# Turning the gated expert products by DMA instead of TensorE in a six-stage transformer block on one core

## The chip, the cores and the metric

One core of a Trainium2 chip runs the whole program. The metric is device time in microseconds (us), the median of three executions. The engines are TensorE (PE, matrix products and transposes into PSUM, with PEld for its weight loads), VectorE (DVE), ScalarE (ACT), GpSimd (POOL) and SyncE (SP, which only issues transfers here). They run their own instruction lists and meet at semaphores.

## The reference, cut to what matters

Six stages follow each other on 2048 tokens of 128 numbers: a ternary feed-forward stage, attention, feed-forward, a mixture of experts, a second attention, and the mixture of experts once more. The change touches only the two mixtures. Each token goes to its two best of eight experts, weighted by a softmax `w` over the two logits:

```python
xs = X[:, :, None, :] * w[..., None]
for e in range(E):
    h = silu(einsum('btsd,dh->btsh', xs, W1[e])) * einsum('btsd,dh->btsh', xs, W3[e])   # H = 512
    y = einsum('btsh,hd->btsd', h, W2[e])
    out = out + where(topi == e, y, 0).sum(axis=2)
```

## The kernel before

**Precision.** Every float32 operand of a product is split into a float16 high part and a float16 low part (the float32 value less the high part), and a product is three matmuls: high by high, high by low, low by high.

**Tiles.** In each mixture (called `moe(0)` and `moe(1)`) the 4096 token copies are sorted by expert into tiles of 128 rows. With padding there are `ETILES` = 46 tiles, 23 for each half of the tokens (`HT`), so 92 tiles in all. GpSimd gathers the rows of a tile from `x_rows` in HBM (L835) and scatters its results into `y_rows` (L843). The expert of a tile is read into registers.

**A tile's path.** (1) `gather` fills `XG`, a ring of 4. (2) `turned_token`, L2103: TensorE turns it; ACT (L1116) and DVE (L1652) write high and low parts. (3) `up`, L1698 to L1700: six matmuls of 512 columns, three into bank 1 (the W1 product), three into bank 2 (W3). (4) `gate`, L1124: ACT writes silu of bank 1 to `SA`; `product`, L1662: DVE multiplies bank 2 by it and writes float32 `G32`, 128 tokens by 512. (5) `turned_product`, L2128: four float32 transposes on TensorE put the product into bank 3 or 4, since `down` needs the 512 hidden numbers on partitions. (6) `product_high` (ACT, L1130) and `product_low` (DVE, L1668) split it out of PSUM. (7) `down`, L2140 to L2142: twelve matmuls of 128 columns into bank 5. (8) `result`, L1138: ACT copies it to `YS`, a ring of 4, and GpSimd scatters it.

**Order.** Each engine's list is written by hand. `run_tiles` goes through turns; in turn `t` a stage with lag `k` handles tile `t-k`, by `TLAGS = (0, 1, 2, 3)`: token, up and gate and product, turned product and split, down and result. So TensorE's turn is token(t), up(t-1), turned product(t-2), down(t-3). GpSimd's turn `u` is gather(u), then scatter(u-8). `carried` adds other work to a turn: the rest of the feed-forward stage, routing of the second half of the tokens, and, in turns 24 to 38 of `moe(0)`, `second_turned`, which turns weights of the second attention.

**SP's list.** It loads weights, writes normed tokens to `x_rows` (L610) and, when a half is scattered, reads `y_rows` back in four transfers (L618).

Of the kernel before, what the change touches and what calls it, by code (L numbers as in the profile page):

```python
# [19 lines left out]
F32 = mybir.dt.float32  # L20
# [11 lines left out]
def macaron_block(nc: bass.Bass, ins, out, phases):  # L32
    tokens = ins["L0_attn_tokens"]
    NB, SEQ, D = tokens.shape
    P = 128
# [32 lines left out]
    with ctx:  # L68
# [74 lines left out]
        GRING = 3  # L143
        XRING = 4
        YRING = 4
# [79 lines left out]
        YS = carve([YRING, D], F32)  # L225
# [7 lines left out]
        GL = carve([GRING, HB, P], F16)  # L233
        G32 = carve([2, H], F32)
        GH = carve([GRING, HB, P], F16)
# [137 lines left out]
        s_gt_ps = sem("gt_ps")  # L373
# [4 lines left out]
        s_y_out = [sem("y_out0"), sem("y_out1"), sem("y_out2"), sem("y_out3")]  # L378
# [4 lines left out]
        def moved(m, slot, t):  # L383

            return 16 * (m * ((ETILES + XRING - 1 - slot) // XRING) + (t + XRING - 1 - slot) // XRING)
# [146 lines left out]
        TLAGS = (0, 1, 2, 3)  # L532
        OUT_LAG = 8

        def run_tiles(m, stages, carried):

            for t in range(ETILES + TLAGS[-1]):
                for f, lag in zip(stages, TLAGS):
                    if f is not None and 0 <= t - lag < ETILES:
                        f(t - lag, ETILES * m + t - lag)  # L540
                carried(m, t)

# [14 lines left out]
        def _(sp):  # L557
# [18 lines left out]
            for i, (src, hi, lo) in enumerate(experts):  # L576
# [12 lines left out]
            sp.wait_ge(s_lo_pool, 2 + 4 * len(experts))  # L589
            flat = stage[:].rearrange("p a b -> p (a b)")  # L590
            sp.dma_start(flat[:, 0:3 * INNER].rearrange("p (c d) -> p c d", d=D), wqkv1).then_inc(s_w1_in, 16)
            sp.dma_start(flat[:, 3 * INNER:4 * INNER], wout1).then_inc(s_w1_in, 16)

            def end_loads():

                for k in range(YRING):
                    sp.wait_ge(s_y_out[k], moved(1, k, ETILES))
# [8 lines left out]
            def moe(n, m):  # L606
                for c in range(NCH):
                    sp.wait_ge(s_ln_xn, NORM_NO[n, c])
                    at = c % HCH * CH
                    sp.dma_start(x_rows[c // HCH][at:at + CH].rearrange("(p t) d -> p t d", t=TPC),  # L610
                                 XN[:, TPC * c:TPC * (c + 1), :]).then_inc(s_x_rows[c // HCH], 16)
                for h in range(PARTS if m == 0 else 1):
                    for k in range(YRING):
                        sp.wait_ge(s_y_out[k], moved(m, k, HT * (h + 1)))
                    for c in range(HCH * h, HCH * (h + 1)):
                        for j in range(TOPK):
                            at = j * TOK + c * CH
                            sp.dma_start(Yt[:, c, j],  # L618
                                         y_rows[at:at + CH].rearrange("(p t) d -> p t d", t=TPC)
                                         ).then_inc(s_y_got[c], 16)  # L620
                    if m == 1:
                        stored(h)

            x_out = out.rearrange("b (t p) d -> p (b t) d", p=P)

            def stored(h):

                for c in range(HCH * h, HCH * (h + 1)):
                    sp.wait_ge(s_x_moe, TOPK * (NCH + c + 1))
                    sp.dma_start(x_out[:, TPC * c:TPC * (c + 1), :], X[:, TPC * c:TPC * (c + 1), :]  # L630
                                 ).then_inc(s_out_done, 16)
            moe(3, 0)
            moe(5, 1)
# [7 lines left out]
        def _(pool):  # L641
# [125 lines left out]
            def attention(a, turns=range(TURNS)):  # L767

                def body(t):
                    p, m, s, v, o = items(t)  # L770
                    if s is not None:
                        j = ITEMS * a + s
                        b = s & 1
                        for u in range(3 if s < ITEMS - 1 else 2):
# [85 lines left out]
        def _(act):  # L860
# [248 lines left out]
            def moe(m):  # L1109
# [8 lines left out]
                def gate(t, w):  # L1118
# [5 lines left out]
                    a_.activation(SA[:, t % 2, :], ps[:, 1, :], ACT.Silu, scale=wup[:, t:t + 1]).then_inc(s_a_sb, 1)  # L1124

                def product_high(t, w):
                    act.wait_ge(s_gt_ps, w + 1)
                    if t >= GRING:
                        act.wait_ge(s_y_ps, w - GRING + 1)
                    a_.activation(GH[:, t % GRING].rearrange("p a b -> p (a b)"), ps[:, 3 + t % 2, :], ACT.Copy  # L1130
                                  ).then_inc(s_g_hi, 1)

                def result(t, w):
                    k = t % YRING
                    act.wait_ge(s_y_ps, w + 1)
                    if t >= YRING:
                        act.wait_ge(s_y_out[k], moved(m, k, t))
                    a_.activation(YS[:, k, :], ps[:, 5, 0:D], ACT.Copy, scale=0.5 / W_UP).then_inc(s_y_sb, 1)  # L1138
                run_tiles(m, (token_high, gate, product_high, result), carried)
# [6 lines left out]
            for k in range(YRING):  # L1146
                act.wait_ge(s_y_out[k], moved(1, k, ETILES))
# [11 lines left out]
        def _(dve):  # L1159
# [488 lines left out]
            def moe(m):  # L1648
# [6 lines left out]
                def product(t, w):  # L1655
# [4 lines left out]
                    if t >= 2:  # L1660
                        dve.wait_ge(s_gt_ps, w - 1)
                    v_.scalar_tensor_tensor(G32[:, t % 2, :], ps[:, 2, :], wup[:, t:t + 1], SA[:, t % 2, :], ALU.mult,  # L1662
                                            ALU.mult).then_inc(s_g32_rdy, 1)

                def product_low(t, w):
                    g = t % GRING
                    dve.wait_ge(s_g_hi, w + 1)
                    v_.tensor_tensor(GL[:, g].rearrange("p a b -> p (a b)"), ps[:, 3 + t % 2, :],  # L1668
                                     GH[:, g].rearrange("p a b -> p (a b)"), ALU.subtract).then_inc(s_g_lo, 1)
                run_tiles(m, (token_low, product, product_low, None), carried)  # L1670
# [498 lines left out]
```

## Time and profile before

| | us |
|---|---|
| median of 3 runs | 967.55 (967.09 to 970.55) |
| span of the profiled execution | 1000.9 |
| `moe(0)`, first gather to last scatter in that span | 360.9 to 530.5 |
| `moe(1)`, its turns from 4 on, to the last scatter | 845.8 to 990.0 |

The page gives no other time of the profiled execution than its span, which is 3.4% above the median of the runs. Times inside the span are compared with the span, and a difference is scaled by 967.55/1000.9 = 0.967 at the end. How to read it: an engine's busy share is an average; in the two mixtures all engines work at once, and what matters is how far apart the tiles follow each other.

### The profile page before, as it was taken

Reading aid. Unit: us, or ns where it says so; the run is one execution under the profiler, and the core shown is the slowest. Engines: PE = TensorE matmul, PEld = TensorE weight load, DVE = VectorE, ACT = ScalarE, POOL = GpSimd, SP = SyncE. Lnnn points to the kernel's source line nnn. Section 1 sums busy time; section 2 is a strip of 40 time slices with the busy share of each in tenths; the row PEclk is TensorE's granted clock in tenths of the full one; section 3 lists DMA queues with packets and bytes.
Section 4 is the critical chain, followed back from the end, with each engine's and each line's share of the span. In section 5 each row is a group of like instructions: output and inputs, shape, how many; then the busy total and the mean of one; then the engine's idle time right before and its main releaser. Section 6 shows DMA issues by size and latency. Waiting matters only on the chain.

```text
span 1000.9 us, 33897 instructions
## 1 busy us (share of the span) xinstructions
PE 897.1 (90%) x13160; PEld 640.5 (64%) x13160; DVE 792.1 (79%) x2394; ACT 673.5 (67%) x1183; POOL 734.7 (73%) x685
## 2 busy tenths in 40 slices
PE   5789999999999879899987899999999985998884
PEld 3467676776777656566654676777677764666663
DVE  6889898888889877777656889888888887866563
ACT  6688888878877626556555787767767762545552
POOL 6789989889887745666545999878888883666662
PEclk9999999999999979999999999999999997999997
DMA  5201011010030001122111000000000001121222
GB/s 153 78 10 45 3 45 45 3 45 2 3 107 3 2 20 39 52 43 85 38 30 51 3 3 3 12 3 2 13 3 3 13 2 30 41 43 44 86 62 82
DMA packets 21118, 33.79 MB, mean 34 GB/s; under 512 B 4578, under 2 KB 10466, under 8 KB 20964
## 3 DMA queue, kind: packets, MB, share of 16 engines
q1 hardware_dynamic: 13728, 18.50, 5.9%
q0 software_dynamic: 5888, 12.07, 4.8%
q8 instruction: 110, 1.80, 0.8%
q10 hardware_dynamic: 1348, 1.05, 0.3%
q14 instruction: 44, 0.36, 0.1%
HBM read 22.44 MB, written 9.18 MB: 32 GB/s over the span
## 4 chain that ended last, share of the span: by engine, by line
PE 63%; DVE 18%; ACT 6%; issue 6%; POOL 3%; another core or an unknown queue 2%; DMA 1%; SPq 0%; POOLq 0%; DVEq 0%; ACTq 0%
PE ps L1698 8%; PE ps L1889 8%; PE ps L1700 8%; PE ps L1699 7%; DVE arena L1308 4%; PE ps L1919 3%; PE ps L2128 3%; PE ps L1853 3%; PE ps L1920 3%; PE ps L1921 3%; PE ps L2140 2%; PE ps L2141 2%; PE ps L2142 2%; PE ps L1864 2%
## 5 line engine op out<-in xcount | busy, mean ns | idle before, releaser
L784 POOL TENSOR_TENSOR arena<-arena 128x1024 f16<-128x1024 f32 x190 | 344.9, 1816 | 86.2 <-ACT arena L980 75.9
L1308 DVE CUSTOM_DVE_ANT_0 arena<-ps,mask_qk 128x512 bf16<-128x512 f32 (+3 forms) x512 | 224.4, 485 | 25.0 <-PE ps L1853 23.8
L972 ACT ACTIVATE arena<-ps,lift 128x1024 f32<-128x1024 f32 (+1 forms) x192 | 186.7, 972 | 85.0 <-PE ps L1899 82.2
L1889 PE MATMUL ps<-arena 64*128 64x512 f16 (+3 forms) x1536 | 148.5, 299 | 10.2 <-ACT arena L972 6.8
L835 POOL DMA_INDIRECT arena<-x_rows,arena x92 | 92.6, 1006 | 88.5 <-PE ps L2103 43.7
L1919 PE MATMUL ps<-arena 128*128 128x65 f16 x1280 | 130.9, 195 | 0.2 <-DVE arena L1332 0.2
L1920 PE MATMUL ps<-arena 128*128 128x64 f16 x1280 | 130.4, 193 | 0.0
L1921 PE MATMUL ps<-arena 128*128 128x65 f16 x1280 | 130.0, 194 | 0.0
L843 POOL DMA_INDIRECT y_rows<-arena x92 | 90.8, 987 | 49.0 <-ACT arena L1138 26.1
L1919 PEld LDWEIGHTS ps<-arena 128*128 128x128 f16 x1280 | 117.4, 98 | 8.4 <-issue 0.5
L1920 PEld LDWEIGHTS ps<-arena 128*128 128x128 f16 x1280 | 117.9, 99 | 0.2 <-issue 0.2
L1921 PEld LDWEIGHTS ps<-arena 128*128 128x128 f16 x1280 | 117.9, 98 | 0.0
L782 POOL CAST arena<-arena 128x1024 f16<-128x1024 f32 x124 | 103.6, 835 | 0.0
L1662 DVE SCALAR_TENSOR_TENSOR arena<-ps,arena 128x512 f32<-128x512 f32 x92 | 68.8, 748 | 29.1 <-ACT arena L1124 16.0
L1889 PEld LDWEIGHTS ps<-arena 64*128 64x128 f16 x1536 | 52.1, 94 | 53.1 <-ACT arena L972 22.3
L1668 DVE TENSOR_TENSOR arena<-ps,arena 128x512 f16<-128x512 f32 x92 | 63.1, 686 | 26.1 <-ACT arena L1130 18.4
L1130 ACT ACTIVATE arena<-ps 128x512 f16<-128x512 f32 x92 | 55.3, 601 | 42.1 <-PE ps L2128 24.7
L2140 PE MATMUL ps<-E2h,arena 128*128 x368 | 71.4, 222 | 11.1 <-DVE arena L1668 6.0
L1124 ACT ACTIVATE arena<-ps,arena 128x512 f32<-128x512 f32 x92 | 63.4, 689 | 18.5 <-PE ps L1700 15.1
L1853 PE MATMUL ps<-arena 64*128 64x512 f16 (+3 forms) x512 | 66.2, 296 | 7.7 <-DVE arena L1308 6.6
L2142 PE MATMUL ps<-E2h,arena 128*128 x368 | 71.1, 219 | 0.0
L2141 PE MATMUL ps<-E2l,arena 128*128 x368 | 71.0, 219 | 0.0
(288 smaller groups left out, 2695.9 us busy)
## 6 DMA issues: line engine op xcount, KB each, us to landing
stage<-in_L_ffn_W SPq DMA_DIRECT2D x4, 1024.0 KB, 5.3
arena<-y_rows SPq DMA_DIRECT2D x14, 256.0 KB, 3.6
x_rows<-XN SPq DMA_DIRECT2D x8, 256.0 KB, 2.1
arena<-x_rows,arena POOLq DMA_INDIRECT x92
y_rows<-arena POOLq DMA_INDIRECT x92
stage<-in_L_attn_Wkv SPq DMA_DIRECT2D x2, 512.0 KB, 8.3
X<-in_L_attn_tokens SPq DMA_DIRECT2D x3, 256.0 KB, 5.1
out_x<-X SPq DMA_DIRECT2D x3, 256.0 KB
```

The lines of the kernel that those rows point to most:

```text
L782: g.tensor_copy(PH[:, b, :, cols], P32[:, :, cols]).then_inc(s_ph_pool, 1)
L784: g.tensor_tensor(PL[:, b, :, cols], P32[:, :, cols], PH[:, b, :, cols], ALU.subtract).then_inc(s_pl, 1)
L835: g.indirect_dma_start(XG[:, t % XRING, :], None, x_rows[t // HT], bass.IndirectOffsetOnAxis(ap=row_i[:, 0, t:t + 1], axis=0)).then_inc(s_ ...
L972: a_.activation(P32[:, :, UNIT_AT[u]:UNIT_AT[u] + UNIT_W[u]], ps[:, 4:6, 0:UNIT_W[u]], ACT.Exp, bias=lift[:]).then_inc(s_ex_p, 1)
L1308: v_.tensor_tensor_reduce(masked[:, x, 0:w], ps[:, 2 + x, at:at + w], mask_qk[:, CH - w:CH], 1.0, NEG, ALU.add, ALU.max, accum_out=MX[:, i ...
L1853: ins_ = mm(ps[:, 2 + x, at:at + (i + 1) * P], QKh[rows, r, 0, i * P:(i + 1) * P], QKh[rows, r, 1, 0:(i + 1) * P], start=(n_ == 0), stop=( ...
L1889: mm(ps[:, 4 + x, at:at + w], keys, queries, start=(n_ == 0 and part == 0), stop=False)
L1919: mm(ps[:, 6 + x, c:c + DH + 1], ph_, VH[:, r, k, x, 0:DH + 1], start=(k == 0), stop=False)
L1920: mm(ps[:, 6 + x, c:c + DH], ph_, VL[:, r, k, x, :], start=False, stop=False)
L1921: ins_ = mm(ps[:, 6 + x, c:c + DH + 1], pl_, VH[:, r, k, x, 0:DH + 1], start=False, stop=(k == i))
L2140: mm(dst, GH[:, g, f, :], wh, start=(f == 0), stop=False)
L2142: ins_ = mm(dst, GL[:, g, f, :], wh, start=False, stop=(f == HB - 1))
```

## The change

The split now comes first and the turn second, and the turn is a transfer. ACT (`product_high`) and DVE (`product_low`) split `G32` from SBUF to SBUF, into `GS`, 128 by 1024 float16, a ring of 3 (`SRING`). SP issues one `dma_start_transpose` per tile, `GS` to `GT`, a ring of 4, 256 KB each. `down` reads `GT`, with a lag of 4 turns instead of 3. Banks 3 and 4, now free, make a second pair for `up` (`up_banks`). `YS` is a ring of 8 instead of 4. SP's list is rewritten so that its other transfers stand between the transposes. GpSimd's list has the same instructions; one wait on the last scatters is added in the second attention.

```diff
-        GRING = 3
+        GRING = 4
+        SRING = 3
-        YRING = 4
+        YRING = 8
...
-        TLAGS = (0, 1, 2, 3)
+        DOWN_LAG = 4
...
+        def up_banks(t):
+            return 1 + 2 * (t % 2), 2 + 2 * (t % 2)
...
+            def results_in(m, h):
+                for k in range(YRING):
+                    sp.wait_ge(s_y_out[k], moved(m, k, HT * (h + 1), YRING))
+                for c in range(HCH * h, HCH * (h + 1)):
+                    for j in range(TOPK):
+                        at = j * TOK + c * CH
+                        sp.dma_start(Yt[:, c, j], y_rows[at:at + CH].rearrange("(p t) d -> p t d", t=TPC)
+                                     ).then_inc(s_y_got[c], 16)
...
+            def moe(m):
+                for t in range(ETILES):
+                    w = ETILES * m + t
+                    sp.wait_ge(s_g_lo, w + 1)
+                    if t >= GRING:
+                        sp.wait_ge(s_y_ps, w - GRING + 1)
+                    sp.dma_start_transpose(GT[:, t % GRING].rearrange("p k f d -> p (k f) d"),
+                                           GS[:, t % SRING].rearrange("p k h -> p (k h)")
+                                           ).then_inc(s_g_turned[t % GRING], 16)
...
+                    if t == 31:
+                        results_in(m, 0)
...
                 def product_high(t, w):
-                    act.wait_ge(s_gt_ps, w + 1)
-                    if t >= GRING:
-                        act.wait_ge(s_y_ps, w - GRING + 1)
-                    a_.activation(GH[:, t % GRING].rearrange("p a b -> p (a b)"), ps[:, 3 + t % 2, :], ACT.Copy
+                    act.wait_ge(s_g32_rdy, w + 1)
+                    if t >= SRING:
+                        act.wait_ge(s_g_turned[(t - SRING) % GRING], moved(m, (t - SRING) % GRING, t - SRING + 1))
+                    a_.activation(GS[:, t % SRING, 0], G32[:, t % 2, :], ACT.Copy).then_inc(s_g_hi, 1)
...
-                run_tiles(m, (token_high, gate, product_high, result), carried)
+                run_tiles(m, ((token_high, 0), (product_high, 2), (gate, 1), (result, DOWN_LAG)), carried)
...
                 def product_low(t, w):
-                    v_.tensor_tensor(GL[:, g].rearrange("p a b -> p (a b)"), ps[:, 3 + t % 2, :],
+                    v_.tensor_tensor(GS[:, t % SRING, 1], G32[:, t % 2, :], GS[:, t % SRING, 0], ALU.subtract
-                run_tiles(m, (token_low, product, product_low, None), carried)
+                run_tiles(m, ((token_low, 0), (product_low, 2), (product, 1)), carried)
...
-                    if t >= 1:
-                        pe.wait_ge(s_a_sb, w)
+                    if t >= 2:
+                        pe.wait_ge(s_a_sb, w - 1)
...
-                def turned_product(t, w):
-                    for f in range(HB):
-                        ins_ = nc.tensor.transpose(ps[:, 3 + k, f * P:(f + 1) * P], G32[:, k, f * P:(f + 1) * P], ident[:])
...
                 def down(t, w):
-                    pe.wait_ge(s_g_lo, w + 1)
+                    pe.wait_ge(s_g_turned[g], moved(m, g, t + 1))
...
-                run_tiles(m, (turned_token, up, turned_product, down), carried)
+                run_tiles(m, ((turned_token, 0), (up, 1), (down, DOWN_LAG)), carried)
```

TensorE's list in a turn of `moe(1)` before: token, the six up matmuls, the four transposes of the product, and then the first of the down matmuls (`arena` holds all tile buffers, `ps` is PSUM).

```order
L2103 MATMUL ps<-ident,arena 128x128 [waits t_lo,xg_in2]
L1698 ISA [waits a_sb,t_lo]
L1698 MATMUL ps<-E1h,arena 128x512
...
L1700 MATMUL ps<-E1h,arena 128x512
L1698 REGISTER_ALU [waits g32_rdy]
L1698 MATMUL ps<-E3h,arena 128x512
...
L1700 MATMUL ps<-E3h,arena 128x512
L2128 MATMUL ps<-ident,arena 128x128 [waits g_lo,g32_rdy]
L2128 MATMUL ps<-ident,arena 128x128 x3
L2140 REGISTER_ALU [waits y_sb,g_lo]
L2140 MATMUL ps<-E2h,arena 128x128
```

The same turn in the changed kernel:

```order
L2156 MATMUL ps<-ident,arena 128x128 [waits t_lo,xg_in2]
L1751 ISA [waits a_sb,t_lo]
L1751 MATMUL ps<-E1h,arena 128x512
...
L1753 MATMUL ps<-E1h,arena 128x512
L1751 REGISTER_ALU [waits g32_rdy]
L1751 MATMUL ps<-E3h,arena 128x512
...
L1753 MATMUL ps<-E3h,arena 128x512
L2185 REGISTER_ALU [waits y_sb,g_turned2]
L2185 MATMUL ps<-E2h,arena 128x128
```

The four L2128 rows are gone, the waits on `a_sb` and `g32_rdy` are now for the tile before the last, and `down` waits for a transfer (`g_turned`).

SP's list through `moe(0)` and the read-back of its results before:

```order
L610 DMA x_rows<-XN 128x512 [waits ln_xn] x4
L618 DMA arena<-y_rows 128x512 [waits y_out2,y_out3,y_out1,y_out0]
L618 DMA arena<-y_rows 128x512 x3
```

And in the changed kernel:

```order
L665 DMA_TRANSPOSE arena<-arena 128x8x128 [waits g_lo] x4
L665 DMA_TRANSPOSE arena<-arena 128x8x128 [waits y_ps,g_lo]
L608 DMA x_rows<-XN 128x512 [waits ln_xn]
L665 DMA_TRANSPOSE arena<-arena 128x8x128 [waits y_ps,g_lo] x3
L608 DMA x_rows<-XN 128x512 [waits ln_xn]
L665 DMA_TRANSPOSE arena<-arena 128x8x128 [waits y_ps,g_lo] x24
L618 DMA arena<-y_rows 128x512 [waits y_out4,y_out5,y_out3,y_out6,y_out2,y_out7,y_out1,y_out0]
L618 DMA arena<-y_rows 128x512 x3
L665 DMA_TRANSPOSE arena<-arena 128x8x128 [waits y_ps,g_lo] x14
```

46 transposes now stand in this list, and the read-back of the first half is issued ahead of the last 14 of them.

## Rows read from the trace of the kernel before

**Rows 1.** The page: busy time of the engines over the span.

```profile
PE 897.1 (90%) x13160; PEld 640.5 (64%) x13160; DVE 792.1 (79%) x2394; ACT 673.5 (67%) x1183; POOL 734.7 (73%) x685
```

**Rows 2.** Stretches: busy us of each engine, granted clock, DMA share, GB/s.

```profile
440.00:493.00 53.00, 49.36 (x419) 35.34 (x418) 35.99 (x72) 31.17 (x77) 34.11 (x35) 1.00 0.21 63
882.00:969.00 87.00, 78.40 (x647) 54.27 (x645) 52.03 (x101) 45.80 (x113) 55.65 (x57) 1.00 0.23 59
...
850.00:860.00 10.00, 9.06 (x96) 6.53 (x95) 9.25 (x39) 5.66 (x13) 4.85 (x5) 1.00 0.12 35
```

**Rows 3.** Timeline of POOL: start, duration, line, idle before and releaser.

```profile
360.87 1.23 POOL L835 DMA_INDIRECT arena<-x_rows,arena  x1 [11.57 <-DVE arena L1515]
...
433.82 0.97 POOL L835 DMA_INDIRECT arena<-x_rows,arena  x1 [1.64 <-DVE arena L1515]
...
440.02 0.97 POOL L835 DMA_INDIRECT arena<-x_rows,arena  x1 [1.38 <-remote]
...
492.75 0.98 POOL L835 DMA_INDIRECT arena<-x_rows,arena  x1 [0.82 <-PE ps L2103]
...
498.33 0.24 POOL L661 TENSOR_SCALAR pw<-mv 128x4 f32<-128x4 f32 x1 [3.32 <-DVE mv L1177]
...
882.48 0.97 POOL L835 DMA_INDIRECT arena<-x_rows,arena  x1 [0.97 <-PE ps L2103]
...
902.79 0.99 POOL L843 DMA_INDIRECT y_rows<-arena  x1 [0.30 <-issue]
904.08 0.97 POOL L835 DMA_INDIRECT arena<-x_rows,arena  x1 [0.30 <-issue]
905.35 0.99 POOL L843 DMA_INDIRECT y_rows<-arena  x1 [0.30 <-issue]
...
968.87 1.11 POOL L835 DMA_INDIRECT arena<-x_rows,arena  x1 [0.30 <-issue]
...
989.06 0.96 POOL L843 DMA_INDIRECT y_rows<-arena  x1 [0.75 <-ACT arena L1138]
```

**Rows 4.** The chain that ended last, end of `moe(1)`: start, duration, what.

```profile
968.37 1.44 PE ps L1700
969.85 2.14 another core or an unknown queue
972.01 0.61 ACT arena L1130
...
976.25 0.44 PE ps L2128 x4
978.77 0.44 PE ps L2128 x4
981.29 0.44 PE ps L2128 x4
```

**Rows 5.** DVE, ACT and TensorE by line, medians of one.

```profile
L2103 PE MATMUL ps<-ident,arena x92: 272/299/454, 364.2 to 979.7; 128*128 128x128 f32 x92
L1130 ACT ACTIVATE arena<-ps x92: 588/597/633, 374.9 to 985.3; 128x512 f16<-128x512 f32 x92
L980 ACT ACTIVATE arena<-arena x64: 1045/1048/1082, 52.3 to 820.7; 128x1024 f16<-128x1024 f32 x64
L1668 DVE TENSOR_TENSOR arena<-ps,arena x92: 677/690/694, 375.5 to 985.9; 128x512 f16<-128x512 f32 x92
L1327 DVE TENSOR_TENSOR arena<-arena x2: 681/681/681, 352.6 to 829.2; 128x512 f16<-128x512 f32 x2
```

**Rows 6.** The page's issues: KB each, median us to landing.

```profile
arena<-y_rows SPq DMA_DIRECT2D x14, 256.0 KB, 3.6
x_rows<-XN SPq DMA_DIRECT2D x8, 256.0 KB, 2.1
...
stage<-in_L_attn_Wout SPq DMA_DIRECT2D x1, 512.0 KB, 8.9
```

**Rows 7.** The page's DMA queues: packets, MB, share of 16 engines.

```profile
q1 hardware_dynamic: 13728, 18.50, 5.9%
...
q8 instruction: 110, 1.80, 0.8%
```

More of the change, by code:

```diff
@@ L224, in macaron_block @@
         used[0] = ARENA - 1024
-        YS = carve([YRING, D], F32)
         tile_ei = carve([64], I32)
@@ L530, in macaron_block @@
         KEY_AT = {k: UNIT_AT[u] + at for u, unit in enumerate(EXP_UNITS) for k, at in unit}
-        TLAGS = (0, 1, 2, 3)
+        DOWN_LAG = 4
         OUT_LAG = 8
         def run_tiles(m, stages, carried):
-            for t in range(ETILES + TLAGS[-1]):
-                for f, lag in zip(stages, TLAGS):
-                    if f is not None and 0 <= t - lag < ETILES:
+            for t in range(ETILES + DOWN_LAG):
+                for f, lag in stages:
+                    if 0 <= t - lag < ETILES:
                         f(t - lag, ETILES * m + t - lag)
                 carried(m, t)
+        def up_banks(t):
+            return 1 + 2 * (t % 2), 2 + 2 * (t % 2)
         def second_weights(i):
@@ new lines, in attention, with body @@
+            def attention(a):
+                def body(t):
+                    if a == 0 and t == 0:
+                        expert_block(0)
+                    if a == 0 and t == 1:
+                        expert_block(1)
+                    if a == 0 and t in (6, 10, 14, 18):
+                        expert_block((t - 6) // 4 + 2)
+                    if a == 0 and t == 27:
+                        second_layer()
+                    if t in ROWS_OUT[a]:
+                        rows_out(*ROWS_OUT[a][t])
+                run_items(body, range(TURNS))
@@ L604, in end_loads @@
                              ).then_inc(s_out_done, 16)
[L606 to L622, printed above, removed]
@@ L624, in _, with stored @@
-            x_out = out.rearrange("b (t p) d -> p (b t) d", p=P)
[L626 to L633, printed above, removed]
+            x_out = out.rearrange("b (t p) d -> p (b t) d", p=P)
+            def stored(c):
+                sp.wait_ge(s_x_moe, TOPK * (NCH + c + 1))
+                sp.dma_start(x_out[:, TPC * c:TPC * (c + 1), :], X[:, TPC * c:TPC * (c + 1), :]
+                             ).then_inc(s_out_done, 16)
@@ L634, in _ @@
+            attention(0)
+            moe(0)
+            results_in(0, 1)
+            attention(1)
+            moe(1)
             end_loads()
@@ L773, in body @@
                         b = s & 1
+                        if a == 1 and s == 1:
+                            for k in range(YRING):
+                                pool.wait_ge(s_y_out[k], moved(0, k, ETILES, YRING))
                         for u in range(3 if s < ITEMS - 1 else 2):
```

79 lines of the change are left out of this document (47 added, 32 removed).

## The prediction

> **What bounds the kernel now.** I read the page first. TensorE is busy 90% of the span [rows 1], which invites the thought that 368 transposes off TensorE are worth their full time. The stretches come next. In the two quiet stretches of the mixtures, 440 to 493 and 882 to 969, TensorE is busy 93% and 90%, GpSimd 64%, DVE 68% and 60%, and the clock is full [rows 2]. So TensorE leads, but it is no plain TensorE bound, and the pace per tile says more.
>
> GpSimd's timeline gives that pace, since it gathers each tile once. From the gather at 882.48 to the last at 968.87 there are 28 steps, 3.09 us each; from 440.02 to 492.75 there are 17, 3.10 each [rows 3]. Two floors lie below. TensorE's undisturbed pace is the step of the L2128 group near the end of the chain: 976.25, 978.77, 981.29, or 2.52 us [rows 4]. GpSimd's own floor is a scatter, a gather and their gaps with nothing to wait for: 902.79 to 905.35, or 2.56 us [rows 3]. **So the kernel sits 0.5 us per tile above two floors that are almost equal.** The 0.5 us comes from stalls. The chain shows one: after L1700, 2.14 us of "unknown queue", before ACT's L1130 [rows 4]. I counted seven of this kind in `moe(1)`, about every fifth tile, and near each the instruction queue (110 fetches of 16 KB [rows 7]) moved a packet. Because the engines are tied closely (one bank pair, the turned product one turn after it is made), a stall of TensorE passes on to all, and at a 2.52 pace against 2.56 on GpSimd nothing can be caught up.
>
> **The change part by part.**
>
> *Removed: four transposes a tile.* Their group takes 0.44 us on TensorE's path [rows 4]. TensorE's floor becomes 2.52 - 0.44 = 2.08. The full price over 92 tiles would be 40 us, but GpSimd's 2.56 is untouched: its list is the same. So in steady stretches the new pace is GpSimd's 2.56, not 2.08, and the gain is 3.09 - 2.56: the slack of 0.48 lets TensorE catch up after a stall, which it could not do before.
>
> *ACT and DVE.* The high split reads SBUF: half of L980's 1048 ns for twice the columns is 524, against 597 for L1130; I take 560, between them [rows 5]. The low split becomes what L1327 does, 681 against 690 for L1668 [rows 5]. Both are hidden: with all four operations a turn costs about 1.8 us on either engine.
>
> *Added: a 256 KB transposing transfer per tile.* The trace of before has none. The bounds are 2.1 us to landing for the same bytes out of SBUF, and 8.9 us for 512 KB, so 4.45 for 256 [rows 6]. I take 3.6, the row of the same size that writes into SBUF. Time allowed: the low split of tile t-2 is done about 1.4 us into turn t, and `down` of that tile begins about 1.5 us into turn t+2 (token 0.2, up 1.3). That is two turns and a little, 5.2 us at 2.56. So 3.6 us is hidden with 1.6 to spare. Without the cover each us beyond 5.2 would cost half a us per tile, since it lies across two turns. Load on the DMA engines: q1 moved 18.5 MB in 5.9% of 16 engines' span [rows 7], so 256 KB takes 0.8 us of all sixteen; per 2.56 us that adds 0.33 to a share of 0.2 [rows 2]. The engines stay under 0.6.
>
> *Moved: SP's list.* Ahead of the transposes stand the four read-backs at t = 31 in each mixture and single `x_rows` writes. The scatters for which the read-backs wait are issued two turns earlier, so the wait is short. What is queued behind them is the next transpose, and TensorE's `down` behind that. Four read-backs of 256 KB add three landings' worth of bytes, about 3 x 1.1 us, against 1.6 to spare: 1.8 us, and twice that is 3.6; I take 4.
>
> *Second bank pair, `YS` ring of 8.* These only remove waits; they are part of the catching up. A ring of 8 lets ACT's result go on although a scatter lands late.
>
> *One more turn of lag.* It costs only at the ends, and is in the tail below.
>
> **The sum** (against the span of 1000.9):
> - `moe(1)` from 882.48: 28 steps from 3.09 to 2.56 (72 us instead of 86.4): -14.4. Lower bound 0, if the stalls stay on the path.
> - `moe(1)` tail: now 989.06 - 968.87 = 20.2 us from the last gather to the last scatter [rows 3], since TensorE is a ring of four tiles behind GpSimd. After, TensorE has kept up. The tile lands after 3.3 (first gather 360.87, first L2103 364.2 [rows 3, 5]), then token, `up` in the next turn, to 6.9; gate, product and both splits with gaps, 3.1; transfer 3.6; down, result, 1.1: 14.7. So -5.4.
> - `moe(1)` before 882: DVE has the routing and is busy 9.25 of 10 us [rows 2]; little can move. -2 (0 to -5).
> - `moe(0)`, 440 to 493: TensorE also turns weights here (one group of four, 0.44, per two turns: 0.22). Its floor is 2.08 + 0.22 + one stall of 2.14 per six tiles, 0.36, so 2.7, which exceeds GpSimd's 2.56. 17 x 0.4 = -6.8.
> - `moe(0)`, first half: 433.82 - 360.87 over 23 tiles is 3.17 [rows 3], with feed-forward and routing in between. Full price of the transposes 23 x 0.44 = 10; half of it, since DVE's routing decides when the second half may start (L1515 released both ends [rows 3]): -5 (0 to -10).
> - `moe(0)` end: GpSimd waited 3.3 us for DVE's L1177 because it ran four tiles ahead [rows 3], and TensorE's backlog is smaller: -4 (0 to -8).
> - read-backs ahead of transposes: +4 (0 to +10).
>
> Together -33.6 on the span, 967.3; times 0.967 is -32.5 on the median, so **935**. All gains at full, costs at nothing: about -49, or 920.
>
> **A page against it.** The landing of 2.1 to 3.6 us for 256 KB [rows 6] is for plain transfers. The Trainium skill, "VectorE: DVE Perf Modes", section "The three transpose paths", gives 390 ns for a 128 x 128 turn on TensorE and 1309 ns by the DMA crossbar. By an estimate from that page, eight such blocks one after another are 10.5 us a tile, and the sum would be about 680 us above the time of now. The same notes, "Advanced Engine Details and Errata", section "X-Bar Transpose (TRN2)", call transposing DMAs as fast as regular ones; by that my 3.6 would stand. No run so far shows either.
>
> **The rivals.**
> - *A, the forecast* (0.50): GpSimd's pace; 918 to 946.
> - *B, the stalls stay* (0.17). Transposes put 0.33 more load on the queues that also fetch TensorE's instructions. If a stall grows from 2.14 to 4 us, TensorE's pace is 2.08 + 4/6 = 2.75 and over 60 quiet tiles 11 us of the gain are lost; with the full cost of the read-backs another 6. About 951, span 946 to 962. For it: the fetch near each stall. Against: 0.48 us of slack a tile absorbs 2.14 in five tiles.
> - *C, no change* (0.08): the pace is set by something that neither floor shows, and a tile's longer path eats the rest; 963 to 972. The case that the change does not do what it says lies here too: the TensorE instructions are gone from its list, so only the gain can fail.
> - *D, slower* (0.25): the crossbar serves one tile after another, slower than tiles are made. Place: SP's queue; `down` waits on `g_turned`, then ACT's `product_high` for its ring of 3. Price: at 4.45 us a tile (the bound from 8.9 for 512 KB [rows 6]) 92 x (4.45 - 3.1) = +124, times 0.967: 1087. It decides from a pace of about 3.1 us on: below that A's gain only shrinks. For it: no row shows a transposing transfer, and each turned block ends as 256 bytes on every partition. Against: an ordinary 256 KB takes 0.8 us of the engines [rows 7]. The Trainium skill's block-by-block estimate above is the extreme of this case.
>
> **How the numbers follow.** 935 is A's value; A's own range is 918 to 946. Half of 1% is about what a measurement tells from no change. Faster by more than 0.5% are A and B and a sliver of C: 0.67. Within: 0.08. Slower: 0.25, of which I put about 0.1 below 1000. The range 916 to 1000 leaves out some 0.03 below and 0.15 above.
>
> **What would show it.** Right: gathers 2.56 to 2.6 apart in the quiet stretches, with "issue" before them and not L2103; TensorE idle about a fifth there; transposes landing within 5 us; scatter of the last tile about 15 us after the last gather. Wrong: TensorE or its `down` line waiting for the transfer (D), ACT's high split waiting for `g_turned` (D), steps still near 3 us with stalls of over 2 us in the chain (B), or a new releaser in front of GpSimd's gathers (C).

## The result and the profile after

The changed kernel takes 975.32 us (median of 8 runs, 969.81 to 978.13) against 968.18 for the kernel before on the same chip (8 runs). The ratio is 1.0068, 95% interval 1.0046 to 1.0090: **slower by 0.7%**, where 935 was forecast. The profiled execution has a span of 972.8 us and took 974.55.

The page of the changed kernel: engines (busy us, share), DMA queues (packets, MB, share of 16 engines), the costliest groups, and an issue row. They answer to [rows 1, 7, 6].

```profile
PE 862.8 (89%) x12792; PEld 599.9 (62%) x12792; DVE 788.3 (81%) x2394; ACT 672.1 (69%) x1183; POOL 742.9 (76%) x685
...
q1 hardware_dynamic: 110880, 42.63, 20.6%
...
L889 POOL DMA_INDIRECT arena<-x_rows,arena x92 | 94.6, 1028 | 50.9 <-issue 23.7
...
L2185 PE MATMUL ps<-E2h,arena 128*128 x368 | 74.4, 226 | 27.0 <-DMA arena<-arena 20.3
...
arena<-y_rows SPq DMA_DIRECT2D x14, 256.0 KB, 4.3
```

GpSimd's gathers now mostly wait for "issue", as forecast; but `down` (L2185) waits 20.3 us for the turned product, in places where TensorE has nothing else. The turning made 110880 packets of q1 out of 13728.

The line of the transfer, SP's L665: min, median and max of SP's own time for one issue in ns, and who waited for it (us, times).

```profile
L665 SPq DMA_TRANSPOSE arena<-arena x92: 1231/1233/3457, 376.1 to 956.0; - x92
...
  PE ps L2185: 20.3, 16
```

Stretches of the changed kernel, columns as in [rows 2]. The first is the quiet one, the others are short ones near its end.

```profile
870.00:928.00 58.00, 48.73 (x391) 30.73 (x390) 36.37 (x66) 31.90 (x83) 43.54 (x43) 0.96 0.86 167
...
926.00:930.00 4.00, 3.73 (x20) 2.23 (x21) 0.98 (x2) 1.70 (x4) 2.36 (x3) 0.57 0.82 191
939.00:943.00 4.00, 4.00 (x23) 2.25 (x23) 1.56 (x4) 1.65 (x4) 2.31 (x3) 0.62 0.89 187
```

The DMA engines are 86% busy. The second and third rows are granted clocks of 0.57 and 0.62, that is, mostly the lower of TensorE's two levels (1.2 against 2.4 GHz). The chain that ended last says what went before each: start, duration, what.

```profile
920.05 6.10 DMA arena<-arena
926.15 0.12 issue
926.27 0.26 PE ps L2185
...
927.93 0.43 PE ps L1751
928.35 0.43 PE ps L1752
...
932.53 0.60 DVE arena L1721
933.15 5.33 DMA arena<-arena
938.49 0.12 issue
...
953.92 2.72 DMA arena<-arena
```

The low split (L1721) ends, the transfer lands 5.33 us later, and `down` follows. Behind a landing of 6.10 us TensorE runs `up` at 0.43 us a matmul instead of 0.22. A late transfer near the end, when the gathers are over, takes 2.72. The chain shows only the late ones. By the semaphores of the trace, the transfers issued between 862 and 930 us land after 2.8 to 6.2 us, 3.9 in the middle (median).

GpSimd's timeline, columns as in [rows 3]:

```profile
894.35 0.97 POOL L889 DMA_INDIRECT arena<-x_rows,arena  x1 [0.30 <-issue]
895.63 0.99 POOL L897 DMA_INDIRECT y_rows<-arena  x1 [0.30 <-issue]
896.92 0.97 POOL L889 DMA_INDIRECT arena<-x_rows,arena  x1 [0.30 <-PE ps L2156]
...
941.65 0.97 POOL L889 DMA_INDIRECT arena<-x_rows,arena  x1 [0.30 <-issue]
944.25 0.98 POOL L897 DMA_INDIRECT y_rows<-arena  x1 [1.63 <-ACT arena L1192]
...
960.70 0.97 POOL L897 DMA_INDIRECT y_rows<-arena  x1 [1.28 <-ACT arena L1192]
```

Where nothing is late, gathers are 2.57 us apart. The tail from last gather to last scatter is 19.05 us, not the 14.7 of the sum.

### The profile page after: what moved, and what is told of

It reads as the page before. It is cut to its first block, busy times and chain, and to the rows that moved or that the text cites. A ratio compares the mean times of both kernels' runs of the same rounds, so it can differ in the third digit from the quotient of the medians.

```text
span 972.8 us, 33253 instructions
## 1 busy us (share of the span) xinstructions
PE 862.8 (89%) x12792; PEld 599.9 (62%) x12792; DVE 788.3 (81%) x2394; ACT 672.1 (69%) x1183; POOL 742.9 (76%) x685
## 3 DMA queue, kind: packets, MB, share of 16 engines
q1 hardware_dynamic: 110880, 42.63, 20.6%
## 4 chain that ended last, share of the span: by engine, by line
PE 56%; DVE 21%; DMA 8%; ACT 6%; issue 6%; POOL 3%; SPq 0%; POOLq 0%; DVEq 0%; ACTq 0%
PE ps L1942 8%; PE ps L1751 7%; DMA arena<-arena 7%; PE ps L1752 6%; PE ps L1753 6%; DVE arena L1362 4%; PE ps L1972 4%; PE ps L1906 3%; PE ps L1973 3%; PE ps L1974 3%; PE ps L2185 2%; PE ps L2186 2%; PE ps L1917 2%; PE ps L1982 2%; DVE arena L1721 2%
## 5 line engine op out<-in xcount | busy, mean ns | idle before, releaser
L897 POOL DMA_INDIRECT y_rows<-arena x92 | 95.0, 1033 | 55.2 <-ACT arena L1192 37.2
L889 POOL DMA_INDIRECT arena<-x_rows,arena x92 | 94.6, 1028 | 50.9 <-issue 23.7
L2185 PE MATMUL ps<-E2h,arena 128*128 x368 | 74.4, 226 | 27.0 <-DMA arena<-arena 20.3
L1192 ACT ACTIVATE arena<-ps 128x128 f32<-128x128 f32 x92 | 25.5, 277 | 79.2 <-PE ps L2187 73.7
L1721 DVE TENSOR_TENSOR arena<-arena 128x512 f16<-128x512 f32 x92 | 63.7, 692 | 15.3 <-ACT arena L1185 15.0
L2187 PE MATMUL ps<-E2h,arena 128*128 x368 | 73.7, 224 | 0.0
L2186 PE MATMUL ps<-E2l,arena 128*128 x368 | 73.5, 223 | 0.1
L2185 PEld LDWEIGHTS ps<-E2h,arena 128*128 128x128 f16 x368 | 36.5, 99 | 50.5 <-issue 41.6
```

Source lines behind the costliest of these rows:

```text
L889: g.indirect_dma_start(XG[:, t % XRING, :], None, x_rows[t // HT], bass.IndirectOffsetOnAxis(ap=row_i[:, 0, t:t + 1], axis=0)).then_inc(s_ ...
L897: g.indirect_dma_start(y_rows, bass.IndirectOffsetOnAxis(ap=row_i[:, 1, t:t + 1], axis=0), YS[:, t % YRING, :], None).then_inc(s_y_out[t % ...
L2185: mm(dst, GT[:, g, 0, f, :], wh, start=(f == 0), stop=False)
```

## The experiments

**The kernel before, profiled again.** No edit; the first on one chip, the second on another.

> The kernel before, unchanged, profiled once more. Theory P (the profiled execution behind the prediction was itself disturbed: about 16 stalls of 2.15 us in the mixtures, 33 us together, are the whole difference between its span of 1000.9 and the median of 968.2): the new span is 966 to 970, and the gathers in the quiet stretches of the mixtures stand about 2.6 us apart instead of 3.1. Rival Q (a profile always stretches this kernel): the span is near 1000 again and the gathers 3.1 apart. Median against before: 1.000 by both.

> The kernel before, unchanged, for one more profile, hopefully on a chip where its time is near 968 (the last chip gave 1008 for the same kernel, with the second attention starting equally long after the first mixture, so that the chips differ in the mixtures alone). Theory C (chips differ): where the median is near 968, the gathers stand 2.7 us apart in the quiet stretches, and the stalls of 2 to 3 us in the chain are few; where it is near 1005, they stand 3.1 to 3.3 apart with such stalls every 5 tiles. Rival P (the profile itself stretches the kernel): gathers 3.1 apart whatever the median.

The first took 1009.59 us beside a before of 1008.29 (ratio 1.0011, 0.9997 to 1.0025), the second 968.40 beside 968.78 (0.9996, 0.9985 to 1.0007). So the kernel before has two prices, by chip. Neither P nor Q of the first expectation had this case: the execution is as long as in the profile of the prediction, and so is the median. Three sets of runs gave 1003.2, 1008.3 and 1009.2 for it; I call where they ran **the 1005 chips**, though all three sets carry one chip number, 12, so it may be a single chip. The result above and two further sets (chips 0 and 3) gave 968; I call these **the 968 chips**. The profile shown ahead of the prediction, span 1000.9, looks like one of a 1005 chip, while the three times beside it are of a 968 chip.

Stretches of the kernel before on a 968 chip:

```profile
435.00:485.00 50.00, 47.95 (x425) 35.04 (x424) 37.71 (x74) 34.23 (x76) 32.54 (x36) 1.00 0.24 67
...
870.00:928.00 58.00, 55.80 (x504) 40.12 (x503) 38.26 (x70) 37.55 (x88) 42.32 (x45) 1.00 0.26 70
```

And its chain, with the group that gave the floor in [rows 4]:

```profile
912.78 0.44 PE ps L2128 x4
...
915.30 0.44 PE ps L2128 x4
...
917.83 0.44 PE ps L2128 x4
...
920.34 0.44 PE ps L2128 x4
```

TensorE is busy 96% and keeps its 2.52 us step near the end of the stretch. On the 1005 chip the chain of the same kernel is broken instead, as in [rows 4]:

```profile
896.34 0.29 DVE arena L1652
896.63 2.89 another core or an unknown queue
```

No such piece stands in the chain of the kernel before on a 968 chip, whose page has the same 110 instruction fetches as [rows 7]. So those fetches alone, which the prediction suspected, do not make the stall.

This table sets the runs side by side. All of it is from GpSimd's timelines: from the start of the first gather to that of the last scatter of each mixture, and the mean step from the 18th gather of `moe(1)` to its last.

| kernel, chip | `moe(0)` | `moe(1)` | step |
|---|---|---|---|
| before, profile of the prediction | 168.6 | 152.2 | 3.09 |
| before, 1005 chip | 171.1 | 157.0 | 3.28 |
| before, 968 chip | 150.1 | 135.7 | 2.66 |
| changed, 1005 chip (`a_again`) | 173.1 | 158.7 | 3.29 |
| changed, 968 chip | 151.2 | 139.8 | 2.75 |
| `free`, 968 chip | 143.7 | 134.5 | 2.73 |
| `copy_h`, 968 chip | 143.0 | 131.6 | 2.63 |
| `lag5_h`, 968 chip | 148.2 | 141.4 | 2.85 |

Between the mixtures every run of the table has 307 to 310 us. The spans of before in the first and the third row, 1000.9 and 966.7, differ by 34.2 us, and the mixtures by 18.5 and 16.5: they hold all of it, and there is no uniform factor.

**The changed kernel on a 1005 chip.** No edit.

> The changed kernel, unchanged, beside it on the same chip. Both theories: 970 to 978, ratio 1.003 to 1.010; its profile shows transposes landing 5 to 7 us after issue, DMA engines over 0.8 busy in the quiet stretches and gathers 2.57 to 2.65 apart.

1016.48 us, ratio 1.0080 (1.0054 to 1.0105). The ratio is as expected; the time and the step of the gathers (3.29) are those of a 1005 chip. The change costs the same 0.7 to 0.8% on both kinds of chip. One of its waits (engine and line, us, times, longest) has no known releaser, which the view calls "remote"; no profile on a 968 chip has one like it:

```profile
ACT arena L1192 <- remote: 52.4, 22, 4.1
```

It is not the turning that brings it: `copy` below has 54.9 us of it on a 1005 chip.

**The path without a turn.** `free` has no transfer: `down` reads the split product as it lies. Its output is another one, but TensorE, ACT, DVE and GpSimd have the work of the changed kernel.

```diff
-        SRING = 3
+        SRING = 5
...
-                    sp.dma_start_transpose(GT[:, t % GRING].rearrange("p k f d -> p (k f) d"),
-                                           GS[:, t % SRING].rearrange("p k h -> p (k h)")
-                                           ).then_inc(s_g_turned[t % GRING], 16)
...
-                        act.wait_ge(s_g_turned[(t - SRING) % GRING], moved(m, (t - SRING) % GRING, t - SRING + 1))
+                        act.wait_ge(s_y_ps, w - SRING + 1)
...
-                    pe.wait_ge(s_g_turned[g], moved(m, g, t + 1))
+                    pe.wait_ge(s_g_lo, w + 1)
...
-                        mm(dst, GT[:, g, 0, f, :], wh, start=(f == 0), stop=False)
+                        mm(dst, GS[:, g, 0, f * P:(f + 1) * P], wh, start=(f == 0), stop=False)
...
```

> The changed kernel without any transposing transfer: down reads the split product as it lies (not turned, so the output is not the reference's), from a ring of 5, with the lag of 4 turns, two bank pairs and the ring of 8 kept; SP issues nothing per tile. It is what the change would give if turning cost nothing at all. Theory G (GpSimd's pace and stalls bound the mixtures already, so TensorE's transposes were nearly free): ratio to before 0.985 to 1.000, a gain of at most 15 us. Rival F (transposes on TensorE cost their full 0.44 us a tile and the transfer gives it back): ratio 0.96 to 0.965, a gain of 35 to 40 us.

961.15 us beside 968.78, ratio 0.9921 (0.9903 to 0.9939). A turn that costs nothing at all is worth 7.6 us here; the transfer takes that back and 7 more. The waits of `free` in `moe(1)`:

```profile
POOL arena L882 <- issue: 12.0, 40, 0.3
POOL y_rows L890 <- issue: 11.6, 38, 0.3
...
PE ps L2149 <- DMA arena<-x_rows,arena: 9.7, 16, 1.7
```

This is theory G of the expectation. TensorE now waits for gathered rows, and GpSimd mostly for nothing ("issue"; its waits for ACT and TensorE are 6.9 and 4.1 us): GpSimd's pace and the landing of its gathers are the bound, as in A of the prediction. But its gathers take 1040 ns each between 862 and 930, against 968 in the kernel before, so the step there is 2.73, and before already had 2.66. The gain is in `moe(0)`, where TensorE also turns weights (143.7 against 150.1).

**The same bytes, not turned.** `copy` moves each product by the same list and the same waits, as a plain transfer. The output is another one.

```diff
-                    sp.dma_start_transpose(GT[:, t % GRING].rearrange("p k f d -> p (k f) d"),
-                                           GS[:, t % SRING].rearrange("p k h -> p (k h)")
-                                           ).then_inc(s_g_turned[t % GRING], 16)
+                    sp.dma_start(GT[:, t % GRING].rearrange("p k f d -> p (k f d)"),
+                                 GS[:, t % SRING].rearrange("p k h -> p (k h)")
+                                 ).then_inc(s_g_turned[t % GRING], 16)
```

> The changed kernel with a plain copy of the same 256 KB from SBUF to SBUF in place of each transposing transfer, so that the down products get operands that are not turned and the output is not the reference's. Theory X (the crossbar transfer is dearer than its bytes: about 1050 packets and 1.5 us of all 16 engines each): the DMA share in the quiet stretches falls from 0.86 to 0.5 or less, landing falls from 5 to 6 us to 2 to 3, down no longer waits, and the time falls to about 960. Rival V (the bytes alone do it): DMA share over 0.75 still and the time within 2 us of the changed kernel.

> The changed kernel with a plain copy of the same 256 KB in place of each transposing transfer (operands not turned, output not the reference's), for a chip where before takes 968. On the slower chip it was 4.7 us faster than the changed kernel. Theory X (the transposing transfer's load, a quarter more than twice the engines' time of a copy, makes down wait): most of the 14 us between the changed kernel (975) and the one without any transfer (961) comes back, time 962 to 967. Rival V (the bytes and the longer path alone): 970 or more.

> The changed kernel with plain copies in place of the transposing transfers (output not the reference's), again for a chip where before takes 968. Theory X (the crossbar transfer's load): 962 to 967. Rival V (bytes and path alone): 970 or more.

On 1005 chips 1011.80 (ratio 1.0041, 1.0023 to 1.0058) and 1008.82 (1.0054, 1.0036 to 1.0072); on a 968 chip 958.07 beside 968.15, **ratio 0.9912** (0.9885 to 0.9939), 4 us below the 962 to 967 of theory X. The times of the first two expectations were meant for a 968 chip. The last one separates the causes: with the longer path, the lag, the rings, SP's rewritten list and every byte in place, the kernel is as quick as `free`. What is left of the loss, 0.9912 to 1.0068 or 15 us (some 3 either way, by the two intervals), belongs to the turning of the transfer on a 968 chip. On a 1005 chip it is less: `copy` and the changed kernel, in one set, are 1.0041 and 1.0080, or 4.7 us apart. There the plain copy keeps a loss of its own, which no run explains. From the page of `copy_h`, the queue:

```profile
q1 hardware_dynamic: 26976, 42.63, 12.9%
```

The line of its transfer, columns as above:

```profile
L665 SPq DMA_DIRECT2D arena<-arena x92: 464/465/772, 374.8 to 939.8; - x92
```

Its waits in `moe(1)`:

```profile
PE ps L2156 <- DMA arena<-x_rows,arena: 7.9, 8, 2.3
...
PE ps L2185 <- DMA arena<-arena: 1.2, 2, 0.7
```

The same 42.63 MB take 12.9% of the engines instead of 20.6%. Less the 6.2% of 966.7 us which q1 has in the kernel before on a 968 chip, and over 92 tiles, that is 0.69 us of all sixteen engines for a plain transfer and 1.53 for a turning one. The median landing between 862 and 930 is 2.4 us. `down` waits 1.2 us in `moe(1)` and 6.3 in the whole kernel (20.3 in the changed one); in `moe(1)` of the changed kernel it is 10.6:

```profile
PE ps L2185 <- DMA arena<-arena: 10.6, 7, 3.2
```

**More time for the transfer.** If only the landing were too late, one more turn of lag would give the loss back.

```diff
-        GRING = 4
-        SRING = 3
+        GRING = 5
+        SRING = 4
-        YRING = 8
+        YRING = 6
...
-        DOWN_LAG = 4
+        DOWN_LAG = 5
```

> The changed kernel with one more turn for the transfer: down has a lag of 5 turns, rings of 5 turned and 4 split products (YS ring 6). Theory L (TensorE's down waits because the transfer takes longer than two turns, and the cold clock after such waits costs too): the waits on the transfer fall from 20 us to under 5 and the time drops by 5 to 10 us, to about 967. Rival T (throughput: the DMA engines or GpSimd's pace bound the mixtures, latency does not): within 2 us of the changed kernel, or 2 us slower for the extra turn at each end.

> The changed kernel with a lag of 5 turns once more (rings of 5 turned and 4 split products, YS ring 6), hopefully on a chip where before takes 968. There down waits 20 us for transfers in the changed kernel. Theory L (this wait is part of the loss): ratio to before 0.998 to 1.003, 4 to 8 us better than the changed kernel's 1.0068. Rival T (load, not latency): 1.006 to 1.010 as before. On a chip where before takes 1008 both say 1.0087 again.

> The changed kernel with a lag of 5 turns. On a chip where before takes 968 the changed kernel's down waits 20 us for transfers. Theory L (latency): 966 to 970. Rival T (the DMA engines' load, which a longer lag does not lower): 973 to 977. On the slower chip again 1.008 to before by both.

> The changed kernel with a lag of 5 turns, again for a chip where before takes 968 (it was 1.008 and 1.005 to before on two slower chips). Theory L (the latency of the transfer is the loss): 966 to 970 there. Rival T (the load of the DMA engines): 973 to 977.

On 1005 chips 1015.77, 1014.83 and 1008.72 (ratios 1.0087, 1.0080, 1.0052, each within 0.003); on a 968 chip 972.15 beside 968.15, ratio 1.0035 (1.0023 to 1.0046). Some 3 of the 15 us come back, and on the 1005 chips, where the changed kernel is at 1.0080, nothing clear of noise. The waits in `moe(1)` of `lag5_h`:

```profile
POOL y_rows L897 <- ACT arena L1192: 16.2, 14, 4.4
...
PE ps L2156 <- DMA arena<-x_rows,arena: 13.7, 12, 4.3
...
PE ps L2185 <- issue: 3.3, 3, 1.6
```

No wait of `down` for its transfer is left. In its place TensorE waits 13.7 us for gathered rows, where `copy_h` has 7.9 and the changed kernel 2.0; GpSimd's gathers take 1088 ns each between 862 and 930, in `copy_h` 991. A piece of its chain:

```profile
861.02 0.29 ACT arena L1192
...
861.39 0.99 POOL y_rows L897
862.38 0.30 issue
862.68 4.88 DMA arena<-x_rows,arena
...
867.61 0.33 PE ps L2156
...
868.33 0.43 PE ps L1752
```

Lateness of the transfer was one part of the loss. Two things can stand behind the rest. One is load: by the semaphores of the traces, a gather issued between 862 and 930 lands after 2.9 us in `free`, 3.2 in `copy_h`, 3.7 in the changed kernel and 3.8 in `lag5_h` (medians; the longest here 8.0). So the turning transfers slow the gathers at either lag. The other is in the edit itself: the scatter still runs eight turns behind its gather, while its result now comes a turn later, so it can hold up the next gather, as in the piece above (result, scatter, gather, token). GpSimd's longest wait for a result is 4.4 us, against 1.9 in the changed kernel and in `copy_h`. No run had a lag of 5 with the scatter moved as well, so the two are not told apart. Neither expectation, lateness alone or load alone, fits by itself.

**The transfer in two halves**, the high part as soon as it is there (`lag5` besides):

```diff
-                    sp.wait_ge(s_g_lo, w + 1)
+                    sp.wait_ge(s_g_hi, w + 1)
...
+                    for k in range(2):
+                        if k == 1:
+                            sp.wait_ge(s_g_lo, w + 1)
+                        sp.dma_start_transpose(GT[:, t % GRING, k], GS[:, t % SRING, k]
+                                               ).then_inc(s_g_turned[t % GRING], 16)
...
```

> The same with a lag of 5 and the transfer of a tile in two, the high part issued when it is ready and the low part after it (128 KB each). Theory L: waits for transfers vanish, the time is that of the single transfer with lag 5 or 1 to 2 us less. Rival T: two issues of 1.2 us on SP per tile and twice as many transfers load the queue more, 2 us slower or more.

1025.73 us, ratio 1.0161 (1.0125 to 1.0196): worse than whole transfers with the same lag in the same set (1.0080), as rival T had it. Each half costs SP as much to issue as a whole one, 1264 ns, so 2.5 us a tile. That this is what made it slower was not separated.

**One bank pair.** The changed kernel with `up` in banks 1 and 2 only, as before.

```diff
-            return 1 + 2 * (t % 2), 2 + 2 * (t % 2)
+            return 1, 2
...
-                    if t >= 2:
-                        pe.wait_ge(s_a_sb, w - 1)
+                    if t >= 1:
+                        pe.wait_ge(s_a_sb, w)
```

> The changed kernel with one bank pair for up, as before, so that up of a tile waits for gate and product of the tile before. If the second pair lets TensorE run ahead of ACT and DVE, this costs 5 to 15 us against the changed kernel; if TensorE waits for the transfer or for gathered rows anyway, it costs under 3.

978.72 us, ratio 1.0108 (1.0090 to 1.0126). The second pair is worth some 4 us, between the two cases of the expectation; it is not what costs.

**Gathers taken out.** Only the first four tiles of a mixture and the first of its second half are gathered, the others compute on old rows (other outputs): in the kernel before, in `free`, and in the changed kernel.

```diff
+        def gathered(t):
+            return t < XRING or t % HT == 0
...
+                    if not gathered(t):
+                        return
...
```

> The kernel before with only the first 4 gathers of each mixture and the first of each half (tile 23); the other tiles read rows left in the ring, so the output is not the reference's. Theory G (before, TensorE at 2.52 us a tile and GpSimd at 2.56 bind together): taking GpSimd's part away alone brings almost nothing, 0 to 6 us. Rival (GpSimd binds before as well, by more than the trace tells): 10 us or more.

> The kernel before with the few gathers alone (output not the reference's). On the slower chip it took 971, 38 us less than before there. Theory S (the two chips differ by stalls that come with the gathers, and TensorE's 2.52 us a tile is the floor of either): on a chip where before takes 968, 963 to 969, a gain of 0 to 5 us. Rival (GpSimd's gathers bound this kernel on every chip): 20 us or more off.

> No transposing transfer (down reads the split product as it lies) and only the same few gathers: TensorE's list without the four transposes, and GpSimd with scatters alone; output not the reference's. Theory G: with GpSimd's floor gone too, TensorE's 2.08 us a tile shows, and the mixtures' quiet tiles fall to 2.1 to 2.2 us: ratio to before 0.955 to 0.970, 30 to 43 us off, against 7.6 us for the free turn alone and nothing much for the gathers alone. Rival D (DVE or ACT with 1.8 us of work and their chain bound it): ratio 0.98 to 0.99.

> No transposing transfer and the few gathers alone (output not the reference's). On the slower chip 945.4. By theory S it is 940 to 945 on a chip where before takes 968 too: the time does not depend on the chip once the gathers are gone. Against the 961 of the kernel without the transfer that gives 16 to 21 us to GpSimd's pace. Rival: it falls by the chips' 38 us as well, to 910.

> The changed kernel with only the first 4 gathers of each mixture and the first of each half (tile 23); the other tiles read rows left in the ring, so the output is not the reference's. GpSimd then has 1.28 us of issue per tile instead of 2.56. Theory G (GpSimd's pace bounds the changed kernel): the mixtures fall from 2.75 to 2.3 us a tile or less, 25 to 40 us off, ratio to before 0.965 to 0.98. Rival T (the transfers and what waits for them bound it): less than 10 us off, ratio over 0.995.

On 1005 chips the kernel before without gathers takes 971.26 and 971.21 (ratios 0.9630 and 0.9679, intervals of 0.002 about them), `free` without gathers 945.43 and 945.11 (0.9368 and 0.9416). The changed kernel without them takes 964.28 on a 968 chip (0.9940, 0.9920 to 0.9961). So on a 1005 chip the gathers cost the kernel before 32 to 38 us, where theory G expected 0 to 6. That leaves it near where a 968 chip has it with its gathers; and two sets that disagreed by 6 us with gathers agree within 0.1 without, with no stall of unknown cause left in the chain. The 1005 chips' extra time comes with the gathers. Without them and without a turn, TensorE leads again. A stretch of `free` without gathers:

```profile
865.00:925.00 60.00, 57.45 (x506) 37.07 (x505) 46.86 (x87) 42.00 (x106) 26.52 (x27) 1.00 0.17 58
```

It is busy 57.45 of 60 us. So, as far as two kinds of chip can be compared, `free` loses about 16 us to the gathers, by GpSimd's pace or by their landing (961 against 945).

The changed kernel gains 12 us without gathers, not the 25 to 40 of theory G: the gathers are not its main bound. With them gone it is still some 19 us slower than `free` without them (964 against 945, again on two kinds of chip), and `down` still waits 5.4 us for its transfer in `moe(1)`. So the turn costs its time also where it can slow no gather.

## Why the prediction was wrong, point by point

**The step that failed first is the one from the trace to "0.5 us per tile above two floors that are almost equal".** The two floors were right: 2.52 for TensorE and 2.56 for GpSimd appear in both traces. The height above them was not that of the timed chip. It was read from one execution of 1000.9 us and scaled by 0.967, although the 33 us between span and median were not spread evenly: they lay in the two mixtures alone. The stretch of 28 steps was 86.4 us in that trace, 83.5 after scaling, and 74.5 on a 968 chip (861.16 to 935.63 in the kernel before profiled again). So of the term of -14.4 only 74.5 - 72 = 2.5 us could ever be had. The kernel before, at 96% TensorE, was bound by its 2.52 us list with few stalls. That GpSimd would be the next bound was right (at 2.73 in `free`, not 2.56, since its gathers took longer), and makes the whole prize small: 7.6 us (`free`), not 32.5.

**Removed, four transposes.** The mechanism was right. The 0.44 us per tile buy only what GpSimd leaves.

**Added, the transfer: mis-sized.** Allowed were 5.2 us, and in the quiet part of `moe(1)` waits stand where the landing takes 5.0 to 6.1. Assumed were 3.6 for all. The middle landing is near that, 3.9; what was missing is the spread under load, from 2.8 to 6.2, since one late tile stops TensorE and an early one gives nothing back. Load was to be 0.8 us of sixteen engines a tile and the share under 0.6; measured 1.53 and 0.86. The 0.8 was a plain transfer's (measured here 0.69). What each us too much would cost was said, but no case had a landing a little too long and a load that hits the gathers. Two things were missed besides: TensorE's granted clock falls to its lower level around some of these waits, and gathers land later under the load (3.7 us against 2.9 in `free`). The clock is the smaller part. Past the first 20 us of a mixture and up to its last gather it is low for some three us from 475.7, 875.1, 926.3 and 939.9 (granted 0.50, 0.51, 0.57 and 0.62 in stretches of 3 to 4 us there), and in `copy_h` from 911.0 alone. Half the pace for three more such stretches is at most some 5 of the 15 us, an estimate that leaves the ends of the mixtures out.

**ACT and DVE.** In the changed kernel the high split takes 630 ns (L1185), the low 692 (L1721), against 560 and 681 assumed. Both stand in front of the transfer, so where it is late they are on the chain (L1721 at 932.53) and not hidden.

**Tail of `moe(1)`.** Forecast 14.7. The changed kernel has 19.05, the kernel before on a 968 chip 18.8, and `copy_h` 14.9 and `free` 14.3 (last gather to last scatter). The working was right for a transfer that is in time; the turning one eats exactly this.

**`moe(0)`, 440 to 493.** Over the same 17 steps (26th to 43rd gather) the 2.7 for TensorE with its extra work fits `free` (2.69) and `copy_h` (2.64), against 2.83 before on a 968 chip and 2.94 after the change. From 2.83 the term of -6.8 could never be had either. First half: 64.8 us before on a 968 chip, 63.9 after, so -0.9 instead of -5, near the bound of 0. End of `moe(0)`: -4 was forecast, and from last gather to last scatter it is 19.4 before and 20.9 after.

**Read-backs ahead of the turning transfers, +4.** Their own landing went from 3.6 to 4.3 us. What they cost the transfer behind them was not tried apart.

**The rivals.** B was wrong: on the timed chip there were no such stalls to keep. D named the right side, place and wait (`down` on `g_turned`), but as a plain serial server slower than 3.1 us a tile; SP's issue is 1.23 us and the engines need 1.53, so tiles are not served slower than made. ACT's high split is in no wait for `g_turned` either. What costs is latency and load below that threshold, and it cost 15 us, not 124. D's condition "below that A's gain only shrinks" is the second failed step: A's gain was 8 to 10 us, and shrank past nothing. The outcome lay in the part of 0.1 put between C and 1000. The estimate of 10.5 us for eight blocks in a row rests on the 1309 ns that the Trainium skill gives for one block ("VectorE: DVE Perf Modes", "The three transpose paths"); the trace disagrees with the estimate, 2.72 with little beside it and at most 6.2 between 862 and 930. That transposing DMAs are "as fast as regular DMAs" (the Trainium skill, "Advanced Engine Details and Errata", "X-Bar Transpose (TRN2)") does not fit the runs either: 1.53 against 0.69 us of the engines, and 15 us of the kernel's time.

**What stays open.** Why a 1005 chip stalls for 2 to 3 us with no known releaser, and why only with the gathers, is not shown: the kernel without gathers was not run on a 968 chip. On 1005 chips even the plain copy is slower than before (1.0041, 1.0054), and `free` was not run there. How the 15 us divide between late transfers, clock and load is known only as far as `lag5_h` gives 3 back and the clock can hold some 5; what `lag5_h` would give with its scatters moved too is not known.

## What to carry to other kernels

When the profiled execution differs from the timed median by several per cent, find where the difference lies before pricing anything: a gap to the floors that only the slower one has is no prize. Ask what the next engine's floor leaves of the gain; here two floors 0.04 us apart said that removing 0.44 from one buys almost nothing. A turning DMA is not a copy: price its engine time, its issue and its latest landings under load, not the middle one, and give `copy` (same bytes, not turned) as the experiment that tells them apart.

## What the hardware showed that was not expected

- A turning transfer of 256 KB, SBUF to SBUF, 128 by 1024 float16, makes 1024 packets of 256 bytes (94208 in the 92 transfers), takes work worth 1.53 us of all sixteen DMA engines, and 1.23 us of SP to issue; a plain one of the same bytes 0.69 and 0.465. A half costs SP 1.26 as well.
- A gather beside such transfers lands after 3.7 us instead of 2.9 (medians between 862 and 930).
- The same program takes 968 us on some chips (numbers 0 and 3) and 1003 to 1009 elsewhere (number 12), each set of runs within 0.6% of its median; the whole difference lies in the stages with indirect gathers, and without them 971.2 us are left on number 12.
- After landings of 5 to 6 us for which TensorE waits 2.0 to 3.3 us, its matmuls of 512 columns follow each other by 0.43 us instead of 0.22 for some three us, at once (926.3) or a little later (939.9). A wait of 2.2 us in `copy_h`, ended at 467.7, is not followed by that.
